# Four PSUM banks as one ring in PE's order, for the scores and the small products of a graph attention layer

## What is computed

```python
q = (x @ Wq + bq).reshape(b, m, h, d)            # h = 8 heads, d = 64, m = 1024 nodes
k = (x @ Wk + bk).reshape(b, m, h, d)
v = (x @ Wv + bv).reshape(b, m, h, d)
scores = einsum('bmhd,bnhd->bhmn', q, k) * scale + edge_bias[edges]
scores = leaky_relu(scores, 0.2)
scores = where(edges > 0, scores, -1e9)
attn = softmax(scores, axis=-1)
out = einsum('bhmn,bnhd->bmhd', attn, v).reshape(b, m, h * d) @ Wp + bp
x = layernorm(x + out)
```

## Time and profile before

| | us |
|---|---|
| median of 3 runs | 5732.4 |
| lowest and highest | 5729.77 and 5737.68 |
| the profiled execution, its device time | 5738.21 |
| the span that its profile covers | 5736.3 |
| of that the fourth layer, about | 4250 to 5736 |

### The profile page before, as it was taken

One profiled execution on the slowest core, in us unless ns is written; L12 is line 12 of the kernel. 1 busy time (PEld: TensorE's weight loads), 2 busy tenths in 40 slices (PEclk: granted clock), 3 DMA queues, 4 the chain that ended last, 5 costly groups with the idle time before them and its releaser, 6 DMA issues. The chain is left out here.

```text
span 5736.3 us, 137991 instructions
## 1 busy us (share of the span) xinstructions
PE 5507.1 (96%) x58164; PEld 2210.2 (39%) x58164; DVE 5378.4 (94%) x8071; ACT 5187.1 (90%) x6137; POOL 905.5 (16%) x890
## 2 busy tenths in 40 slices
PE   8999999999999999999999999998879999999998
PEld 2333333333333333333333333333445454454454
DVE  8999999999999999999999999997669999999998
ACT  8999999999999999999999999996868888888887
POOL 0000000000000011111111111111312222223223
PEclk9999999999999999999999999998879999999999
DMA  1000000000000000000000000000521110111110
GB/s 43 20 16 20 20 17 18 20 20 16 20 20 16 20 20 16 20 16 20 20 16 20 16 20 20 16 20 26 168 70 33 36 33 25 33 36 33 33 29 15
DMA packets 144490, 156.45 MB, mean 27 GB/s; under 512 B 51782, under 2 KB 119110, under 8 KB 143878
## 3 DMA queue, kind: packets, MB, share of 16 engines
q1 hardware_dynamic: 143238, 147.55, 9.2%
q10 hardware_dynamic: 640, 0.07, 0.0%
HBM read 137.10 MB, written 2.10 MB: 24 GB/s over the span
## 5 line engine op out<-in xcount | busy, mean ns | idle before, releaser
L254 ACT ACTIVATE a_hidden<-a_B,a_A 128x1024 f32<-128x1024 f32 x3264 | 3485.4, 1138 | 193.3 <-PE apsS L219 189.3
L328 DVE TENSOR_SCALAR a_hidden<-a_B,a_A 128x1024 f32<-128x1024 f32 x4928 | 3555.4, 791 | 106.3 <-PE apsS L219 86.2
L219 PE MATMUL apsS<-a_hidden,a_w_sel 128*32 128x512 f32 x32768 | 3557.9, 593 | 3.0 <-DVE a_hidden L328 3.0
L219 PEld LDWEIGHTS apsS<-a_hidden,a_w_sel 128*32 128x32 f32 x32768 | 1045.5, 110 | 2412.5 <-issue 2048.8
L610 PE MATMUL m3S<-xT,Q 64*128 64x512 f32 x2048 | 596.7, 657 | 133.8 <-ACT x_even L654 90.4
L626 PE MATMUL m3O<-ZT,Xr 32*64 32x256 f32 x16384 | 579.6, 415 | 4.3 <-DVE ZT L703 4.3
L654 ACT ACTIVATE x_even<-m3S,bias 128x512 f32<-128x512 f32 x684 | 434.3, 689 | 142.8 <-PE m3S L610 120.5
L626 PEld LDWEIGHTS m3O<-ZT,Xr 32*64 32x64 f32 x16384 | 359.8, 142 | 319.0 <-issue 218.5
L703 DVE STREAM_TRANSPOSE ZT<-x_even 128x1024 f32<-128x1024 f32 x342 | 421.6, 1236 | 55.2 <-ACT x_even L663 50.9
L694 DVE CUSTOM_DVE_ANT_0 x_even<-x_even,mask 128x1024 f32<-128x1024 f32 x342 | 440.4, 1322 | 6.4 <-ACT x_even L654 6.3
L663 ACT ACTIVATE x_even<-x_even,low 128x1024 f32<-128x1024 f32 x342 | 394.0, 1152 | 0.0
(11 more groups left out here) (157 smaller groups left out, 3056.2 us busy)
## 6 DMA issues: line engine op xcount, KB each, us to landing
a_adj_in<-adj SPq DMA_DIRECT2D x128, 512.0 KB, 3.6
adj_in<-adj SPq DMA_DIRECT2D x128, 512.0 KB, 4.1
Xr<-x_odd SPq DMA_DIRECT2D x128, 64.0 KB, 2.5
out<-yn SPq DMA_DIRECT2D x64, 32.0 KB, 1.5
x_even<-x SPq DMA_DIRECT2D x1, 256.0 KB, 2.8
wqT<-L_wqT SPq DMA_DIRECT2D x1, 130.0 KB, 4.3
wkT<-L_wkT SPq DMA_DIRECT2D x1, 130.0 KB, 4.4
wvT<-L_wvT SPq DMA_DIRECT2D x1, 130.0 KB, 4.4
```

Of the source, the lines that this page charges most:

```text
L219: last = pe.matmul(psS[k % 2][32 * q:32 * q + 32, h * HALF:(h + 1) * HALF], w["sel"][layer][:, 30 - 2 * p:62 - 2 * p], hidden[:, (k * GROU ...
L254: act.activation(hidden[:, (k * GROUPS + p) % SLOTS, q, :], B2[:, g % 2, :], ACT.Relu, bias=A2[:, g % 2, pair:pair + 1]).then_inc(hid_act, 1)
L328: dve.tensor_scalar(hidden[:, (k * GROUPS + p) % SLOTS, q, :], B2[:, g % 2, :], A2[:, g % 2, pair:pair + 1], 0.0, ALU.add, ALU.max).then_i ...
```

## The change

The three score banks and the one for aux jobs become one ring of four. A list `users` is built in PE's order: two entries for the scores of a slot, one for each aux job. The user at position n gets bank n mod 4, and before writing PE waits until the user four positions earlier has been read: by ACT (`leaky_ready`) if it was a score, by DVE (`aux_out`) if it was an aux job. ACT and DVE read from the bank that the list gives. `row_term` and `query` now wait for `turn_x` by name, which the removed wait on the aux job before had covered.

```diff
-        psS = [ctx.enter_context(nc.psum_tensor(f"m3S{i}", [P, HALF], F32)) for i in range(3)]
+        ring = [ctx.enter_context(nc.psum_tensor(f"m3S{i}", [P, HALF], F32)) for i in range(4)]
         psO = ctx.enter_context(nc.psum_tensor("m3O", [P, 4, HALF], F32))
-        psA = ctx.enter_context(nc.psum_tensor("m3A", [P, HALF], F32))
...
-        order = list(first)
+        order, users = list(first), [(job,) for job in first]
         for i in range(U + 3 * PAIRS):
-            order += aux_jobs(i, 0) + aux_jobs(i, 1)
+            for gap in range(2):
+                if i < U:
+                    users += [(i, gap, 0), (i, gap, 1)]
+                order += aux_jobs(i, gap)
+                users += [(job,) for job in aux_jobs(i, gap)]
         place = {job: i for i, job in enumerate(order)}
+        spot = {user: i for i, user in enumerate(users)}
         done = lambda *job: place[job] + 1
+        bank = lambda *user: ring[spot[user] % 4]
...
+            def bank_free(spots):
+                earlier = [users[at - 4] for at in spots if at >= 4]
+                scored_there = [4 * u[0] + 2 * u[1] + u[2] for u in earlier if len(u) == 3]
+                made_there = [done(*u[0]) for u in earlier if len(u) == 1]
+                if scored_there:
+                    pe.wait_ge(leaky_ready, max(scored_there) + 1)
+                if made_there:
+                    pe.wait_ge(aux_out, max(made_there))
+
             def aux(job):
                 what, b, i = job
-                if place[job]:
-                    pe.wait_ge(aux_out, place[job])
+                bank_free([spot[(job,)]])
+                psA = bank(job)
+                if what in ("row_term", "query"):
+                    pe.wait_ge(aux_out, done("turn_x", b, 1))
...
-                at = 4 * k + 2 * half
-                if at >= 2:
-                    pe.wait_ge(leaky_ready, at - 1)
+                bank_free([spot[(k, half, e)] for e in range(2)])
                 for e in range(2):
                     rows = slice(C * e, C * e + C)
-                    last = pe.matmul(psS[(at + e) % 3][:, :], Q[rows, t % 2, h, :],
+                    last = pe.matmul(bank(k, half, e)[:, :], Q[rows, t % 2, h, :],
```

More of the change, by code:

```diff
@@ L653, in leaky @@
                     act.wait_ge(turned, 2 * (k - 3) + e + 1)
-                act.activation(Z(k, e)[:, half * HALF:(half + 1) * HALF], psS[(4 * k + 2 * half + e) % 3][:, :], ACT.Prelu,
+                act.activation(Z(k, e)[:, half * HALF:(half + 1) * HALF], bank(k, half, e)[:, :], ACT.Prelu,
                                bias=bias[:, b % 2, head:head + 1], scale=-HEAD_SLOPE * w["scale"],
```

## The result

The ring takes 5984.4 us (median; 5980.0 to 5984.9) against 5731.1 us before: 1.0438 times the time, 95% interval 1.0425 to 1.0451. That is 253 us slower. The forecast was 5914 us with a range of 5850 to 5970: the direction and the places were right, the change was 71 us larger than forecast, and the time lies outside the range.

The account below looks back on a forecast made before the run. A loop of PE, ACT and DVE, with DVE full in the fourth layer's undisturbed tile, bounds the kernel. 61 x (2.47 loops + 0.45 clock) = 178, plus 4 at the ends, 182 on 5732.4: 5914 us, range 5850 to 5970.

Parts of the forecast that it names:

- That only waits move, and which: Per tile, PE's 1.98 us ACT wait goes; slot 3 waits for the query's copy-out, slot 7 for the project product.
- The wait for `turn_x`: A turn_x in slot 7 holds the next tile's slot 1, but is copied out before PE arrives: cost nothing.
- The loops: Two loops starting and ending on DVE lengthen the fourth layer's full-clock tile from 21.23 to 23.70 us: +2.47 us.
- clean tile: Undisturbed fourth-layer tile of 21.23 us, eight half-steps numbered slots 0 to 7; DVE busy 20.99 us, no room.
- (b): Slot 3's scores wait until DVE has copied the query out, 1.58 us after they had started before.
- loop b: Query copy-out through scores 3 and 4 to step 1's transpose: 6.63 us against 5.57 of DVE work; DVE idles 1.06.
- The clock: After a 3.4 us PE pause the clock falls in nearly every tile, costing 1.5 us instead of 1.05: +0.45.
- loop c: Project product through scores 7 and 0 to the transpose: 6.20 us against 4.79 of DVE work; DVE idles 1.41.
- The rival of the clock falling twice a tile: Both DVE loops hold and the clock falls twice a tile, price 3.0 instead of 1.5: 6000 us; chance 0.06.
- the query's wait alone counts: PE late in slot 7 anyway, so the product's wait costs nothing; only the query's counts: 5825 us; chance 0.06.
- Faster: Copy-outs come in time, slot 3's 1.98 us pause goes, clock stays up: 64 us gained, 5668 us; chance 0.03.
- no difference: The new waits fall where PE was waiting anyway: 5732 us; chance 0.02.

Follow-up runs that it names:

- the ring with PE kept busy: The ring, slot 3's first-head score matmul issued four times before the wait for the query's bank, same result each time: 5833.0 us, 1.0177.
- kept busy: First-head score matmul of slot 3 repeated with the same result, only to keep PE at work; in the kernel before, issued twice before the ACT wait: 5665.5 us.
- project's wait alone: Kernel before, three score banks and separate bank kept, with scores of slot 7 waiting until DVE has made the project product: 5837.7 us, 1.0183.
- query's wait alone: Kernel before, three score banks and separate bank kept, with scores of slot 3 waiting until DVE has copied the query out: 5908.0 us, 1.0309.
- the ring with the first head early: The ring, slot 3's first-head score matmul issued once, before the wait for the query's bank, not repeated: 5986.8 us, 1.0447.
- the project's wait and PE kept busy: Kernel before, project's wait added in slot 7, slot 3's first-head score matmul issued twice before the wait for ACT: 5767.7 us, 1.0062.

## Why the prediction was right and wrong

**That only waits move, and which:** right. The three places are those named: the wait for ACT went, the query's and the product's came, 61 and 62 times. The bank order decided it, as the rows of the order ahead of the prediction show, and the experiment with three banks and both waits gives the ring's time within 7 us.

The wait for `turn_x`, costed at nothing, shows as 14 waits of 0.2 us.

**The loops:** right in kind, a little short. Forecast 23.70 us a tile at full clock, 24.01 in the ring with PE kept busy. From the product's scores to the query's scores it is 4466.45 - 4454.53 = 11.92 us, where the sum had 6.20 + 5.44 = 11.64. Two terms failed. DVE's stretch from the transpose to the end of the query is 4465.65 + 0.66 - 4460.68 = 5.63 us, not 5.44: I had got 5.44 by subtraction from the tile's 21.23, as if DVE repeated itself exactly in that tile. It does not; this row of the kernel before, with the transpose of the earlier trace rows, gives 4468.44 + 0.66 - 4463.52 = 5.58:

```profile
4468.44 0.66 DVE L719 TENSOR_TENSOR Q<-m3A,cq 128x512 f32<-128x512 f32 x1
```

And the handover from the copy-out to PE's next scores is 0.14 us here, not 0.06, which had been read at the very start of the layer. In all 0.31 us a tile, 19 us.

One reading was too strong, though it changes neither the tile nor the forecast: that DVE has no room at all in the clean tile. One of its masked minima there runs 2.05 us, beside the building of the mask on POOL:

```profile
4448.94 1.05 POOL L536 TENSOR_SCALAR mask<-adj_in 128x1024 bf16<-128x1024 int32 x1
4449.01 2.05 DVE L694 CUSTOM_DVE_ANT_0 x_even<-x_even,mask 128x1024 f32<-128x1024 f32 x1
```

Sixty minima of the layer take 1.9 to 2.1 us in the kernel before, one a tile, and none in the ring, where POOL builds the mask while DVE waits. So some 0.8 of the 5.57 us that (b) counts as DVE's own work are not work, and DVE idles more than the 1.06 us. In the ring with PE kept busy loop b has 0.73 + 0.99 us of idle time:

```profile
4890.77 0.66 DVE L739 TENSOR_TENSOR Q<-m3S,cq 128x512 f32<-128x512 f32 x1
...
4893.49 1.25 DVE L713 CUSTOM_DVE_ANT_0 x_even<-x_even,mask 128x1024 f32<-128x1024 f32 x1 [0.73 <-ACT x_even L673]
...
4898.04 1.25 DVE L722 STREAM_TRANSPOSE ZT<-x_even 128x1024 f32<-128x1024 f32 x1 [0.99 <-ACT x_even L682]
```

Its length, 4898.04 - (4890.77 + 0.66) = 6.61 us, is the 6.63 of the forecast.

**The clock:** right that it falls in every tile (61 slow stretches in 61 tiles), wrong in its price. Forecast 1.5 us a tile; in the ring it is 26.87 - 24.01 - 0.46 = 2.40 us, and the repeated matmuls, which take the slow stretches away, gain 151 us, 2.5 a tile; PE's own time from scores 3 to scores 4 has 2.21. This is the term that took the time out of the range: 0.9 us a tile, 55 us. With the 19 of the loops that makes 182 + 74 = 256, against 253 measured. The failed step is the sentence that took 1.5 as "close to the measured 1.62". A short slow stretch does cost about 1.6, but the longer pause does not only bring it more often, it brings one of twice the length in two tiles of three (43 of 61), which costs about 2.5. All 43 begin while PE is still waiting, so that all of scores 3 runs slow as well (2.08 us in place of 1.13). The value of 3.0 that I had kept for the price's upper end was meant for a second fall on loop c; the second part came on loop b. The price measured, 2.40, was inside the bounds of 0.8 to 3.0 that the prediction named, but its range took the price only up to 2.1, so the range was too narrow by its own terms. Loop c, with the 1.1 us pause, showed no fall: all 61 follow the pause before slot 3.

**The rival of the clock falling twice a tile,** 6000 us, was nearest in time, and that is luck: the clock falls once a tile, for longer. That the query's wait alone counts was wrong: PE is ready 1.1 us before the product in every tile (forecast 1.0). Faster and no difference did not come. The faster one was to decide by a query drained 1.64 us sooner; with both copy-outs moved up in DVE's order the loss does go, but the time is 5714.7 us and not its 5668.

The Trainium skill, "Perfetto Trace Analysis", section "Matmuls", advises to rotate independent matmul groups through different banks. Here the ring costs 4.4% with the copy-outs late and nothing once they come early (0.9967); that the rotation itself gains anything, no run shows. The Trainium skill, "TensorE: Matmul & The Clock Gate", section "A second HAM failure mode: psum-queue depth-cycling", tells of small pauses of PE between matmul groups with which the clock goes up and down. The traces agree (39 slow stretches before, 61 in the ring) and add a price, 1.1 to 2.5 us a tile; it is the pauses that count, since three banks with both waits added have the ring's time.

The clock's price in the four cases that have a partner with PE kept busy: the tiles with a short and with a long slow stretch, PE's mean time from scores 3 to scores 4 above 2.97 us, the time without and with PE kept busy, and the difference in us and per tile. The partner's first head also starts sooner, so a part of each difference may be that.

| kernel | pauses of PE, us | short, long (of 61 or 62) | above 2.97 | without | kept busy | difference | per tile |
|---|---|---|---|---|---|---|---|
| before | 1.98 | 37, 2 | 1.04 | 5732 | 5665 | 67 | 1.1 |
| project's wait alone | 1.98 and 1.1 or 1.6 | 50, 4 | 1.46 | 5838 | 5768 | 70 | 1.1 |
| query's wait alone | 3.7 | 31, 30 | 2.10 | 5908 | 5771 | 137 | 2.2 |
| the ring | 3.7 and 1.1 | 18, 43 | 2.21 | 5984 | 5833 | 151 | 2.5 |

In three of the four rows PE's own account and the difference agree within 0.3 us. With the project's wait alone a part of the slow time is hidden: the product's pause is 1.1 us in the tiles with a slow stretch and 1.6 in the eight without.

## What to carry to other kernels

A ring in the producer's order ties every user to the reader of the one four places before, so put two readers in one ring only if the slower one drains in time. While DVE's copy-outs were late, the separate bank for them was worth 253 us here and the fourth bank for the scores at most 7. When a wait is added, close the loop it makes (from the engine that releases it back to the same engine), compare it with that engine's own work in between, and take that work from rows, not by subtraction. Price PE's pause with its clock: look first for what stands in front of the instruction that PE waits for, since moving a 1 us copy by two places on ACT gained 1.15% here.

## What the runs showed of the hardware

- The lower clock comes in stretches of two lengths, about 3.4 and about 7 us in the granted clock of the traces. A short one costs PE about 1.6 us between scores 3 and scores 4, a long one 2.5 to 2.7.
- The length of the pause settles neither how often the clock falls nor for how long. After pauses of 1.98 us it fell in 39 of 62 tiles in the kernel before (2 of them long) and in 54 of 62 with the project's wait alone (4 long). After pauses of 3.7 us it fell in every tile, but 43 of 61 were long in the ring and 30 of 61 with the query's wait alone. After pauses of 2.80 us (the ring with the first head early) 40 were long and 15 short, in a kernel that takes as long as the ring (5987 and 5984 us).
- A pause of 1.15 us still brought the fall in 30 of 61 tiles (clock 0.96 in the mean between 4300 and 5700), while in the ring with PE kept busy one of 1.1 us before slot 7, and with the project's wait and PE kept busy one of 1.6 us at the same place, left the clock at 1.00. What PE did before the pause differs (the query, scores 2 and a single head's matmul before slot 3; scores 6 and weigh steps before slot 7); whether that is what matters stays open, no run tells it apart.
- A masked minimum on DVE and the mask building on POOL do not run side by side at full speed. Where the minimum starts 0.07 us after the mask building it takes 2.05 us, in place of some 1.2; where it starts first, the mask building takes 2.0 us in place of 1.05 and the next minimum 2.0 as well. This is read from the timelines; no run moved either of them on purpose.
